# Vision-transformer layer on one core: the attention output turned ahead of the fourth unit, the second QKV product after it

## The chip, the cores and the metric

One core of a Trainium2 chip runs the whole kernel in one launch. The metric is the time of that launch in microseconds (us); the kernel before was run three times: 829.83 us median, 829.82 to 830.21. One execution was profiled.

The engines are named as in the profile: PE (TensorE, matmuls and transposes), PEld (its weight loads), DVE (VectorE), ACT (ScalarE), POOL (GpSimd), SP (SyncE, which issues nearly all DMAs).

## What is computed

32 images of 3 x 224 x 224 are cut into 256 patches each and embedded to 256 features (x). Then one layer follows: attention with a causal mask (16 heads of 16 features, 4 key and value heads) on the normalised x, added to x, and a feed-forward part with quantised activations and weights.

```python
h = tok(x)                                   # patches @ W + b
h = h + attn(layernorm(h))                   # causal, 16 heads, 4 kv heads, rotary positions
h = h + ffn(layernorm(h))                    # int8-like fake quantisation, silu(gate) * up, down
# attn: q, k, v = x@wq, x@wk, x@wv; q, k rotated
#       softmax(mask(q k^T / 4)) v, then @ wo
```

The quantisation scale of the feed-forward part is the largest magnitude over all images, so all images must be through attention before the feed-forward part starts. The change lies in the first part, attention.

## The kernel before

The first part is a pipeline over images, written as one step function for each engine (PE, ACT, POOL, DVE, SP), called for each step x from -3 to 34. Steps 6 to 27 run in a hardware loop, two steps a turn; the others are written out. In one step several images are at work at once: the patch product of image x+3, the QKV product of x+2 (in two halves of 128 tokens), the units of x+1, the first four score pairs of image x and the last four of x-1, and the output product of x-2. Each engine runs its step function in the written order. The engines meet only through semaphores, so an instruction that waits holds up all that stands behind it on its engine.

The work that the change and the prediction name, in the order in which one image meets it:

- *patch* (PE L484): the embedding, two halves of 15 matmuls. ACT scales it and makes a 16-bit high part (L767, L772), DVE the low part of h (L1204), SP turns both by a DMA transpose (L380).
- *QKV product*, `project(x, 0)` and `project(x, 1)` (PE L498): 6 matmuls for each half of the tokens. ACT converts each half (L791), POOL rotates it (L991, L994) and adds (L1004). ACT then makes the maximum stack (L807, L809) and, after one exponential, the score stack (L820 to L822), DVE its low part (L1184, L1186).
- *unit*, `unit_pair` 0 to 5 (PE L516 or L522, and L535), and *maximum*, `reduce_pair` 0 to 5 (DVE L1198): a first pass over the scores that finds each row's maximum. A unit waits for the maximum before it, since they share two banks. The units are here called first to sixth. They need the transposed maximum stack (SP L388).
- *score pair* 0 to 7 (PE L550, L552), and its exponential (ACT L829). All score pairs share one pair of banks, so score pair i waits for the exponential i-1. The first four need the first two of four DMA transposes of the score stacks (SP L400), which in turn wait for all six maxima of that image. The first to fourth are score pairs 0 to 3.
- *mask* (POOL L979) of each exponential, and *attend* 0 and 1 (PE L566, L570): probabilities times values. ACT copies its result out (L837).
- *turn*, `o_turn(x, 0)` and `o_turn(x, 1)` (PE L581): four transposes each of image x-1's attention output into a bank of 512 columns each. DVE takes the reciprocal of the sums (L1237) and divides (L1245): this is `o_sums` and `o_normalise`. ACT makes the high part (L844), DVE the low part (L1263), SP turns both (L410).
- *output product*, `out_project` (PE L591), and the residual (DVE L1255).

Four kinds of job share two banks, `shared[0]` and `shared[1]`. `JOBS` lists them in PE's order, the place in the list modulo 2 gives the bank, and `PLACE` says which image a step does. `take_bank` derives from the list what a job must wait for: the job two places earlier in the list must have been read out.

```python
JOBS = [("patch", 0), ("out", 0), ("qkv", 0), ("qkv", 1), ("o_t", 0), ("o_t", 1)]
PLACE = {("patch", 0): 3, ("out", 0): -2, ("qkv", 0): 2, ("qkv", 1): 2, ("o_t", 0): -1, ("o_t", 1): -1}
```

So before, patch waits for the reading of the turn's first half (the division), out for that of the second half, the second QKV half for the residual, and the turn for the conversions of the QKV product. The division reads both banks at once and counts for both halves.

ACT's order in a step, which the change leaves alone (`late` is the image whose exponentials run; the fourth exponential is `exp_pair(late, 3)`):

```python
exp_pair(late, 0); o_copy(late + -1, 1); values(late); projected(late, 0)
exp_pair(late, 1); projected(late, 1)
exp_pair(late, 2); exp_pair(late, 3)
x_high(early); on_high(late); high(late); exp_pair(late, 4); fill_stack(late)
```

SP's order in a step, unchanged too: load of the next patches, transposes of h (L380), of the attention output (L410), of the maximum stack (L388), four of the score stacks (L400), and the store of h1 (L365).

Of the kernel before, what the change touches and what calls it, by code (L numbers as in the profile page):

```python
# [30 lines left out]
D = 256  # L31
# [81 lines left out]

JOBS = [("patch", 0), ("out", 0), ("qkv", 0), ("qkv", 1), ("o_t", 0), ("o_t", 1)]
PLACE = {("patch", 0): 3, ("out", 0): -2, ("qkv", 0): 2, ("qkv", 1): 2, ("o_t", 0): -1, ("o_t", 1): -1}
PER_IMAGE = {"patch": 1, "qkv": 2, "o_t": 2, "out": 1}

# [1 line left out]
def vit_layer(nc, x_t, w_emb, w_qkv, w_o, w_gate, w_up, w_down, clips, rope, eye, tri, out):  # L121
    with ExitStack() as ctx:
# [332 lines left out]
        def _(pe):  # L455
# [34 lines left out]
            def project(x, tb):  # L490
                z = x + 2
                b = take_bank(z, ("qkv", tb))
                pe.wait_ge(h_turned[z.parity], z.half * 16 + 16)
                if x.known and z.n == 0 and tb == 0:
                    pe.wait_ge(weights_split, 3)
                for c in range(DC):
                    for sx, sw in PARTS:
                        mm = pe.matmul(b[:, 0:QKV_COLS], h_t[:, sx, tb, c, :], wqkv[:, sw, c, :],  # L498
                                       start=(c == 0 and (sx, sw) == PARTS[0]),
                                       stop=(c == DC - 1 and (sx, sw) == PARTS[-1]))  # L500
                mm.then_inc(done["qkv"], 1)
# [82 lines left out]
            def out_project(x):  # L584
                w = x + -1
                b = take_bank(w, ("out", 0))
                pe.wait_ge(on_turned[w.parity], w.half * 16 + 16)
                for tb in range(TB):
                    for c in range(DC):
                        for sx, sw in PARTS:  # L590
                            mm = pe.matmul(b[:, tb * D:(tb + 1) * D], on_t[:, sx, tb, c, :],  # L591
                                           wo[:, sw, c, :], start=(c == 0 and (sx, sw) == PARTS[0]),
                                           stop=(c == DC - 1 and (sx, sw) == PARTS[-1]))
                mm.then_inc(done["out"], 1)
# [38 lines left out]
            def step(x):  # L633
                early, late = x + 1, x + -1
                if (x + 3).exists():
                    patch(early, 0)
                if (x + -1).exists():
                    score_pair(late, 4)
                if x.exists():
                    unit_pair(late, 5)  # L640
                if (x + 3).exists():
                    patch(early, 1)
                if (x + -1).exists():
                    score_pair(late, 5)
                    attend(late, 0)
                    score_pair(late, 6)
                if (x + -2).exists():
                    out_project(late)
                if (x + 1).exists():
                    unit_pair(x, 0)  # L650
                if (x + -1).exists():
                    score_pair(late, 7)
                if x.known and x.n == -2:
                    turn_weights(0)
                if (x + 2).exists():
                    project(x, 0)
                if x.exists():
                    score_pair(x, 0)
                if (x + 1).exists():
                    unit_pair(x, 1)  # L660
                if (x + -1).exists():
                    attend(x + -1, 1)
                if x.known and x.n == -2:
                    turn_weights(1)
                if (x + 1).exists():
                    unit_pair(x, 2)
                if x.exists():
                    score_pair(x, 1)
                if (x + 2).exists():
                    project(x, 1)  # L670
                if x.exists():
                    score_pair(x, 2)
                if (x + 1).exists():
                    unit_pair(x, 3)
                if (x + -1).exists():
                    o_turn(x, 0)
                    o_turn(x, 1)
                if x.known and x.n == -2:
                    turn_weights(2)
                if x.exists():  # L680
                    score_pair(x, 3)
                if (x + 1).exists():
                    unit_pair(x, 4)
# [413 lines left out]
        def _(dve):  # L1097
# [135 lines left out]
            def o_sums(x):  # L1233
                w = x + -1
                dve.wait_ge(done["o_t"], w.n * 2 + 2)
                o = pair[0][:, :].rearrange("p (b h d) -> p b h d", b=TB, h=HEADS)
                dve.reciprocal(sums, o[:, :, :, HD:HD + 1]).then_inc(sums_ready, 1)  # L1237
# [66 lines left out]
            def step(x):  # L1304
# [17 lines left out]
                    norm_stats(early)  # L1322
                if (x + 1).exists():
                    reduce_pair(x, 2)
                if (x + 3).exists():
                    h_low(early)
                if x.known and x.n == -2:
                    quantise_weights(2)
                if (x + 1).exists():
                    reduce_pair(x, 3)  # L1330
                if (x + -1).exists():
                    o_sums(x)
                    o_normalise(x)
                if (x + 1).exists():
                    reduce_pair(x, 4)
                if x.known and x.n == -2:
# [160 lines left out]
```

## Time and profile before

| | |
|---|---|
| median of three runs | 829.83 us |
| profiled execution | 827.3 us |
| its span, first to last instruction | 825.6 us |
| mean granted TensorE clock | 0.954 of full (full is 2.4 GHz) |
| busy: PE, DVE, ACT, POOL | 666.7, 663.3, 586.9, 591.5 us |

The first part takes about 650 us of the span, the feed-forward part the rest. A row of a timeline gives the start and the duration in us, the engine, the line, the operation, the output and the input, how often it is repeated, and in brackets how long the engine sat idle just before and what ended the wait. A duration ends a little after the next instruction of the same engine may start, since they are pipelined.

### The profile page before, as it was taken

What the parts mean: (1) busy time and instruction counts of PE and PEld (TensorE: products, weight loads), DVE (VectorE), ACT (ScalarE), POOL (GpSimd) and SP (SyncE); (2) the same over time, 40 slices, a digit from 0 to 9 for tenths busy, and PEclk for the clock granted to TensorE, in tenths of its full rate; (3) what the DMA queues carried; (4) which work ended last, traced back from release to release, by engine and by line L of the source; (5) the groups of instructions that cost most, each with busy time, mean ns of one, the idle gap of its engine ahead of it and who ended that gap; (6) DMA issues with size and microseconds to landing.
All of it is one profiled execution on the core that took longest, in us unless ns stands there. A gap on an engine that the chain in (4) does not pass through costs nothing. (4 is left out here: it accounts for less than half of the span.)

```text
span 825.6 us, 20928 instructions
## 1 busy us (share of the span) xinstructions
PE 666.7 (81%) x6706; PEld 381.5 (46%) x6706; DVE 663.3 (80%) x1052; ACT 586.9 (71%) x972; POOL 591.5 (72%) x689
## 2 busy tenths in 40 slices
PE   3578888888888888888888888888776369997894
PEld 2344555554555555545555555455333223332563
DVE  5856888888888888888888888888765359999894
ACT  4346677777777777787777777877666258886883
POOL 1456888888888888888888888886654148884363
PEclk9797999999999999999999999999889769999898
DMA  8245666667666655566665655665543212221499
GB/s 278 58 97 114 127 138 135 123 135 138 140 134 146 143 133 121 132 139 140 134 144 144 133 121 132 140 140 103 104 77 62 61 38 52 49 40 25 71 177 160
DMA packets 245384, 96.57 MB, mean 117 GB/s; under 512 B 222432, under 2 KB 240608, under 8 KB 245344
## 3 DMA queue, kind: packets, MB, share of 16 engines
q1 hardware_dynamic: 236896, 87.69, 48.3%
q0 software_dynamic: 8448, 8.39, 6.9%
q8 instruction: 20, 0.33, 0.2%
q14 instruction: 20, 0.16, 0.1%
HBM read 24.74 MB, written 16.78 MB: 50 GB/s over the span
## 5 line engine op out<-in xcount | busy, mean ns | idle before, releaser
L1198 DVE TENSOR_REDUCE act_all<-pair 128x4 f16<-128x1024 f32 (+1 forms) x192 | 234.2, 1220 | 34.5 <-PE pair L535 34.4
L484 PE MATMUL pair<-act_all 128*128 128x256 f16 (+1 forms) x960 | 116.7, 275 | 21.1 <-DVE act_all L1245 18.5
L829 ACT ACTIVATE act_all<-pair 128x768 f32<-128x768 f32 x128 | 103.0, 805 | 32.2 <-PE pair L552 32.2
L979 POOL TENSOR_SCALAR_AFFINE_SELECT ffn<-ffn 128x512 f32<-128x512 f32 x128 | 93.8, 742 | 42.4 <-ACT ffn L829 39.6
L829 ACT ACTIVATE ffn<-pair 128x768 f32<-128x768 f32 x128 | 102.1, 797 | 19.1 <-PE pair L552 19.1
L979 POOL TENSOR_SCALAR_AFFINE_SELECT act_all<-act_all 128x512 f32<-128x512 f32 x128 | 78.4, 633 | 43.2 <-ACT act_all L829 43.2
L484 PEld LDWEIGHTS pair<-act_all 128*128 128x128 f16 (+1 forms) x960 | 90.1, 98 | 40.0 <-issue 22.6
L550 PE MATMUL pair<-act_all 64*128 64x256 f16 x512 | 72.6, 280 | 39.7 <-ACT ffn L829 24.3
L1184 DVE TENSOR_TENSOR act_all<-act_all 128x512 f16<-128x512 f32 x32 | 69.8, 2181 | 41.2 <-ACT act_all L822 41.2
L991 POOL TENSOR_TENSOR act_all<-act_all 128x160 f32<-128x160 f32 x128 | 76.4, 618 | 27.2 <-ACT act_all L791 27.2
L1011 POOL TENSOR_TENSOR act_all<-act_all 128x1280 f16<-128x1280 f32 x31 | 81.4, 2627 | 18.0 <-ACT act_all L781 18.0
L498 PE MATMUL pair<-act_all 128*128 128x384 f16 x384 | 76.4, 337 | 0.0
L1004 POOL TENSOR_TENSOR act_all<-act_all 128x320 f32<-128x320 f32 x64 | 68.1, 1064 | 10.8 <-POOL act_all L994 10.5
L940 ACT ACTIVATE ffn<-pair,gate_scale 128x512 f32<-128x512 f32 x96 | 60.9, 653 | 16.2 <-PE pair L710 9.0
L550 PEld LDWEIGHTS pair<-act_all 64*128 64x128 f16 x512 | 24.9, 93 | 99.5 <-ACT ffn L829 50.6
L837 ACT ACTIVATE act_all<-pair 128x512 f32<-128x512 f32 x64 | 38.0, 593 | 41.6 <-PE pair L570 41.6
L1018 POOL TENSOR_TENSOR act_all<-act_all 128x2 f32<-128x2 f32 x64 | 44.6, 698 | 27.2 <-DVE act_all L1283 19.4
L522 PE MATMUL pair<-act_all 64*128 64x256 f16 x512 | 50.0, 274 | 15.0 <-DVE act_all L1198 13.7
L535 PE MATMUL pair<-act_all,eye_wide 64*128 64x128 bf16 (+1 forms) x768 | 60.3, 236 | 0.0
L807 ACT ACTIVATE act_all<-act_all 128x512 f16<-128x512 f32 x32 | 20.2, 630 | 53.2 <-POOL act_all L1004 53.2
L591 PE MATMUL pair<-act_all 128*128 128x256 f16 x384 | 50.1, 283 | 8.8 <-DMA act_all<-ffn 8.8
L552 PE MATMUL pair<-act_all 64*128 64x128 f16 x512 | 56.9, 219 | 0.0
(135 smaller groups left out, 1510.9 us busy)
## 6 DMA issues: line engine op xcount, KB each, us to landing
act_all<-x_t SPq DMA_DIRECT2D x32, 640.0 KB, 4.2
out<-act_all SPq DMA_DIRECT2D x32, 256.0 KB, 2.6
out<-ffn POOLq DMA_DIRECT2D x16, 512.0 KB, 7.0
act_all<-act_all SPq DMA_TRANSPOSE x192, 3.0
act_all<-w_down SPq DMA_DIRECT2D x1, 704.0 KB, 8.4
act_all<-w_emb SPq DMA_DIRECT2D x1, 640.0 KB, 3.9
ffn<-w_gate SPq DMA_DIRECT2D x1, 640.0 KB, 6.9
ffn<-w_up SPq DMA_DIRECT2D x1, 640.0 KB, 7.5
```

Of the source, the lines that this page charges most:

```text
L484: mm = pe.matmul(b, xs[0:k, sx, c, tb * P:(tb + 1) * P], we[0:k, sw, c, :], start=(c == 0 and (sx, sw) == PARTS[0]), stop=(c == KC - 1 and ...
L498: mm = pe.matmul(b[:, 0:QKV_COLS], h_t[:, sx, tb, c, :], wqkv[:, sw, c, :], start=(c == 0 and (sx, sw) == PARTS[0]), stop=(c == DC - 1 and ...
L535: mm = pe.matmul(on_diagonal, eye_wide[rows, at_:at_ + P], tri_b[rows, rows].rearrange("p (a t) -> p a t", a=1).to_broadcast([64, n_, 64]) ...
L550: pe.matmul(b[:, 0:TOKENS], op[rows, k, 0:P], op[rows, pair_, :], start=True, stop=True)
L829: act.activation(probs[i // 4][:, o:o + 2, 0:3, :].rearrange("p h k s -> p h (k s)"), pair[1][:, :].rearrange("p (h c) -> p h c", h=2)[:, ...
L940: act.activation(silu[m % 3][:, 0:cols], bank[2 + m % 3][:, 0:cols], ACT.Silu, scale=gate_scale[:, m:m + 1]).then_inc(silu_ready, 1)
L979: pool.affine_select(out=p, in_=p, pattern=[[0, 4], [1, P]], compare_op=ALU.is_ge, fill=0.0, base=0, channel_multiplier=-1).then_inc(maske ...
L991: op = pool.tensor_tensor(rot_b[:, at_, :, to], qk_of_qkv[:, at_, :, of], rope_s[:, 1, at_, :, to].to_broadcast([P, 1, QK, 8]), ALU.mult)
L1004: pool.tensor_tensor(qk[:, tb].rearrange("p h d -> p (h d)"), rot_a[:, tb].rearrange("p h d -> p (h d)"), rot_b[:, tb].rearrange("p h d -> ...
L1011: pool.tensor_tensor(x_parts[v.parity][:, 1], xt[v.parity], x_parts[v.parity][:, 0], ALU.subtract).then_inc(x_low_ready, 1)
L1184: dve.tensor_tensor(stack[:, :, 0:HEADS, 32:48], qk[:, :, 0:HEADS, :], stack[:, :, 0:HEADS, 16:32], ALU.subtract)
L1198: dve.tensor_reduce(to, pair[2][:, :].rearrange("p (k g t) -> p k g t", k=2, g=n_), AX.X, ALU.max).then_inc(unit_reduced, 1)
```

## The change

The list of jobs has the second QKV half at its end. With it the turn's first half gets bank 1 and its second half bank 0, so the two halves of the tokens lie in the other order, and the output product reads `1 - tb` to put them right. The turn's first half now waits for the residual, its second half for the conversion of the first QKV half, and the second QKV half for the division; patch waits for the division too, and out for the conversion of the second QKV half. PE's order becomes: score pair 1, turn, score pair 2, fourth unit, second QKV half, score pair 3. On DVE, the reciprocal and the division come before the low part of h and the fourth maximum. ACT, POOL and SP are not touched.

```diff
-JOBS = [("patch", 0), ("out", 0), ("qkv", 0), ("qkv", 1), ("o_t", 0), ("o_t", 1)]
+JOBS = [("patch", 0), ("out", 0), ("qkv", 0), ("o_t", 0), ("o_t", 1), ("qkv", 1)]
@@ out_project
-                            mm = pe.matmul(b[:, tb * D:(tb + 1) * D], on_t[:, sx, tb, c, :],
+                            mm = pe.matmul(b[:, tb * D:(tb + 1) * D], on_t[:, sx, 1 - tb, c, :],
@@ PE, step
                     score_pair(x, 1)
+                if (x + -1).exists():
+                    o_turn(x, 0)
+                    o_turn(x, 1)
+                if x.exists():
+                    score_pair(x, 2)
+                if (x + 1).exists():
+                    unit_pair(x, 3)
                 if (x + 2).exists():
                     project(x, 1)
-                if x.exists():
-                    score_pair(x, 2)
-                if (x + 1).exists():
-                    unit_pair(x, 3)
-                if (x + -1).exists():
-                    o_turn(x, 0)
-                    o_turn(x, 1)
@@ DVE, step
                     reduce_pair(x, 2)
+                if (x + -1).exists():
+                    o_sums(x)
+                    o_normalise(x)
                 if (x + 3).exists():
                     h_low(early)
                 if x.known and x.n == -2:
                     quantise_weights(2)
                 if (x + 1).exists():
                     reduce_pair(x, 3)
-                if (x + -1).exists():
-                    o_sums(x)
-                    o_normalise(x)
```

## Rows read from the trace of the kernel before

**Rows 1.** Waits of PE from 106 to 565 us: who waited for whom, sum, times, longest.

```profile
PE pair L484 <- DVE act_all L1245: 17.4, 25, 0.7
PE pair L550 <- ACT ffn L829: 15.1, 50, 0.4
PE pair L516 <- DVE act_all L1198: 9.5, 21, 0.5
```

**Rows 2.** One step: length; busy PE, PEld, DVE, ACT, POOL (instructions); clock; DMA share, GB/s.

```profile
403.93:422.31 18.38, 16.08 (x185) 9.63 (x184) 15.74 (x27) 14.25 (x25) 15.59 (x20) 1.00 0.60 136
```

**Rows 3.** Timeline of PE in that step: start, duration, engine, line, operation [idle before].

```profile
411.51 0.28 PE L550 MATMUL pair<-act_all 64*128 64x256 f16 x2
...
412.30 0.40 PE L516 MATMUL pair<-act_all 64*128 64x128 f16 x8 [0.45 <-DVE act_all L1198]
...
415.16 1.15 PE L498 MATMUL pair<-act_all 128*128 128x384 f16 x6
416.63 0.28 PE L550 MATMUL pair<-act_all 64*128 64x256 f16 x2 [0.33 <-ACT act_all L829]
...
417.23 1.09 PE L581 MATMUL pair<-act_all 128*128 128x128 f32 x8
418.26 0.28 PE L550 MATMUL pair<-act_all 64*128 64x256 f16 x2
...
418.63 0.39 PE L522 MATMUL pair<-act_all 64*128 64x256 f16 x4
...
419.86 1.80 PE L484 MATMUL pair<-act_all 128*128 128x256 f16 x15 [0.72 <-DVE act_all L1245]
```

**Rows 4.** Timeline of ACT in that step.

```profile
415.30 0.58 ACT L791 ACTIVATE act_all<-pair,act_all 128x384 f32<-128x384 f32 x1
...
418.64 0.81 ACT L829 ACTIVATE act_all<-pair 128x768 f32<-128x768 f32 x1 [0.81 <-PE pair L552]
...
420.50 0.62 ACT L844 ACTIVATE ffn<-act_all 128x512 f16<-128x512 f32 x1
422.69 0.63 ACT L807 ACTIVATE act_all<-act_all 128x512 f16<-128x512 f32 x1 [1.57 <-POOL act_all L1004]
```

**Rows 5.** Timeline of DVE in that step.

```profile
416.27 0.83 DVE L1204 TENSOR_TENSOR act_all<-act_all 128x512 f16<-128x512 f16 x1
...
418.49 0.35 DVE L1237 RECIPROCAL act_all<-pair 128x32 f32<-128x32 f32 x1
418.93 0.69 DVE L1245 TENSOR_TENSOR act_all<-pair,act_all 128x512 f32<-128x512 f32 x1
...
421.16 0.69 DVE L1263 TENSOR_TENSOR ffn<-act_all,ffn 128x512 f16<-128x512 f32 x1 [0.40 <-ACT ffn L844]
```

**Rows 6.** Timeline of POOL in that step: rotation of the second half, and its addition.

```profile
419.30 1.00 POOL L991 TENSOR_TENSOR act_all<-act_all 128x160 f32<-128x160 f32 x2
...
421.29 1.28 POOL L1004 TENSOR_TENSOR act_all<-act_all 128x320 f32<-128x320 f32 x1 [0.17 <-POOL act_all L994]
```

**Rows 7.** Timeline of SP's DMA issues; last, the first two L400 transposes' landing.

```profile
421.88 1.23 SPq L410 DMA_TRANSPOSE act_all<-ffn  x1
423.64 1.42 SPq L388 DMA_TRANSPOSE act_all<-act_all  x1
425.22 5.45 SPq L400 DMA_TRANSPOSE act_all<-act_all  x4
...
DMA to landing us min/median/max: 2.8/2.9/3.0
```

**Rows 8.** Line L1184 of DVE over the whole span, and POOL's masks in that step.

```profile
L1184 DVE TENSOR_TENSOR act_all<-act_all x32: 691/2442/2819, 44.1 to 608.9; 128x512 f16<-128x512 f32 x32
...
422.52 1.81 POOL L979 TENSOR_SCALAR_AFFINE_SELECT act_all<-act_all 128x512 f32<-128x512 f32 x3
```

**Rows 9.** Two long waits late in PE's timeline.

```profile
588.41 0.40 PE L550 MATMUL pair<-act_all 64*128 64x256 f16 x2 [2.62 <-ACT ffn L829]
...
627.91 1.47 PE L591 MATMUL pair<-act_all 128*128 128x256 f16 x12 [1.83 <-DMA act_all<-ffn]
```

More of the change, by code:

```diff
@@ L668, in step @@
                     score_pair(x, 1)
-                if (x + 2).exists():
-                    project(x, 1)
+                if (x + -1).exists():
+                    o_turn(x, 0)
+                    o_turn(x, 1)
                 if x.exists():
@@ L674, in step @@
                     unit_pair(x, 3)
-                if (x + -1).exists():
-                    o_turn(x, 0)
-                    o_turn(x, 1)
+                if (x + 2).exists():
+                    project(x, 1)
                 if x.known and x.n == -2:
```

## The prediction

> **What bounds the kernel now.** The change touches only the first part of the program, the loop over 32 images, so I read there. First, the waits of TensorE in the steady stretch [rows 1]: 25 waits for the division in 459 us, so a step takes 459 / 25 = 18.36 us. Second, one such stretch by engine [rows 2]: TensorE is busy 16.08 us of 18.38 and no other engine over 15.8. No engine is full; TensorE idles 2.3 us in pieces. So the step is set by a ring of waits, and the timelines of the engines show it.
>
> The ring of before: first maximum (VectorE) releases the second unit at 412.30, the second attend follows, ScalarE copies its output, converts the first QKV product (415.30), GpSimd rotates both halves until 422.57, ScalarE's next operation starts at 422.69 and had been free since 421.12 [rows 3, 4, 6]; the fifth exponential, the stack fill, VectorE's low parts and the residual follow, and then the next first maximum. Two things the change touches stand outside it: the patch product waits 0.72 us for the division at 419.86, and the third score pair waits 0.33 us for an exponential at 416.63 [rows 3].
>
> **The change, part by part.** Nothing is added or removed; the turned output's halves change banks and the output product reads them crosswise, which costs nothing (same instructions, same sizes). No DMA is added. Two program orders and three bank waits change.
>
> (1) *The turn comes first.* It takes the place where the second QKV product started, 415.16 [rows 3]. The eight transposes take 1.09 us [rows 3]. The second four now take the bank of the first QKV product, which ScalarE has read at 415.30 + 0.58 = 415.88 [rows 4]. Half of 1.09 plus the drain of one is 0.65: end 416.55. TensorE would then have waited for the exponential until 416.63 anyway, so the turn itself costs nothing here.
>
> (2) *The division.* VectorE is done with the third maximum when its next operation starts, 416.27 [rows 5], so it waits for the turn. Reciprocal at 416.60; the division starts 0.44 later and takes 0.69 [rows 5], ending at 417.73. The low part of h and the fourth maximum are queued behind it, some 1.2 us later each; the next that needs that maximum is the fifth unit, which (4) makes late anyway.
>
> (3) *The product has a new wait.* Its bank is now the one the division reads. The third score pair and the fourth unit in front of it end by 417.23 [rows 3], so TensorE waits for 417.73. Between the division's end (418.93 + 0.69 = 419.62) and the patch product (419.86) lie 0.24 us [rows 3, 5]; I take 0.2. The product runs 417.95 to 419.10, 1.15 us long and 2.8 us later than before (415.16).
>
> (4) *What is queued behind it on ScalarE.* ScalarE's order is not changed: it converts the second product and only then runs the third exponential, which releases the fourth score pair. Conversion at 419.17, 0.58 long; the exponential behind it takes 0.81 [rows 4], so 419.75 to 420.56; the score pair at 420.6 instead of 418.26 [rows 3]. TensorE stands still from 419.10 to 420.6, about 1.5 us: this stall is new. The patch wait of 0.72 goes in return, for the division is long done. From score pair to patch product it was 1.60 with that wait, so 0.88 without: 421.5 instead of 419.86, TensorE 1.6 us late.
>
> How much of this reaches the ring? Three ways lead to the next second unit.
>
> TensorE's own: of the 2.3 us of idle time, 0.72 and 0.33 lie ahead of the patch product; the other 1.25 lie behind it, and of them (15.1 + 9.5) / 25 = 1.0 ahead of the second unit, as waits for exponentials and for the first maximum [rows 1]. 1.6 less 1.0 is **0.6 us a step**.
>
> ScalarE's: the fourth exponential 0.38 after its scores, at 421.0 (before 418.64); the copy of the output's high part 1.86 later (418.64 to 420.50), at 422.84, to 423.46; so the operation that started at 422.69 starts 0.52 behind its start, at 423.35 [rows 4]. GpSimd's second rotation could begin at 419.75 instead of 419.30 [rows 6] and stays covered by this. **0.65 us a step**, straight into the old ring.
>
> SyncE's queue: the low part of the output waits for the high part: 423.5 instead of 421.16 on VectorE, 0.69 us [rows 5], ended 424.2. SyncE issues the output's transpose then (424.24, was 421.88), and it takes the queue for 1.23 us. The transpose for the maximum stack comes behind it and one more check of semaphores: 425.6 instead of 423.64. The four of the score stacks come 1.58 behind that (423.64 to 425.22), 427.2; the second of them at a quarter of 5.45 later, 428.55, and it lands after 2.9: 431.45 [rows 7]. The next first score pair needs it. Before, it started at 411.51 + 18.36 = 429.87 [rows 3], and the same sum gave a landing at 429.5: cover of 0.4 us. Now it starts at 431.5, the second unit 0.37 later (as 418.26 to 418.63), 431.87 against 412.30 + 18.36 = 430.66 [rows 3]: **1.2 us a step**. This is the longest of the three, and it closes on itself: second unit, attend, turn, division, product, conversion, third exponential, output transpose, stack transposes, first score pair. A ring of 19.6 us.
>
> A rule of the skill bears on this term. What the rows show: VectorE's subtraction for the score stack's low parts took 0.69 us at its shortest and 2.44 at the median [rows 8]; in the steady steps GpSimd's long subtraction of the next patches runs beside it, and in the last steps, where it is short, that one is missing. The output's low part, a subtraction of the same kind, moves from 421.16 to 423.5, among GpSimd's three masks of 0.6 us each, which start at 422.52 [rows 5, 8]. The Trainium skill, SBUF — State Buffer, section "SBUF: two separate sides", states that a VectorE instruction with two SBUF inputs and a GpSimd instruction that reads SBUF exclude each other, and the later one waits for the whole of the other. By it the ring would be up to 0.6 us longer, 1.8 instead of 1.2, when a mask has just begun. Without it I keep 1.2 and put 0.3 more into the range.
>
> **The sum.** Steps 1 to 29 have both a turn and a product. 27 of them at 1.2 are 32.4. The last two have no new image to widen between the fourth exponential and the output's high part, so that way is shorter, and steps -1 and 0 move the product behind the fourth unit without a turn: these four lie between 0 and 1.2, I take 0.8 (ScalarE's way costs 0.65 without SyncE's): 3.2. Together 35.6. The last three steps have no QKV product; the turn comes up to 1 us earlier in them, where the output product waits for its transpose; I count 0, at best -1. The profiled execution took 827.3 us (span 825.6), so 862.9; the median of the runs shown, 829.8, lies 2.5 above it: **865 us**, slower by 4.3%.
>
> **The rivals.**
> *Only the short ways count.* If the stack transposes land early enough (their cover is worked out from few rows, and 0.6 us would do it), a step costs 0.6: 27 x 0.6 + 3 = 19, so 849 us. For it: two ways agree on it. Against: SyncE's queue has three transposes behind one late one. Chance 0.2.
>
> *The clock falls.* TensorE's granted clock went from 2.4 to 1.2 GHz around waits of 2.62 us late in the loop, and there a score matmul took 0.40 us instead of 0.28 [rows 3, 9]. Against: a wait of 1.83 us left it up, for the 12 matmuls behind it took 1.47 us, 0.12 each, as the patch product's 15 in 1.80 [rows 3, 9], and the new stall is 1.5. Each fall would double a few us of work, of which perhaps 2 show. One fall in every second or third step adds 18 to 27 to the 865: 883 to 892. Chance 0.1.
>
> *Hidden.* If the third exponential's delay is taken up by waits that I have not seen, nothing changes: 830. Against: the queue orders force the stall, and rows show at most 1.25 us of slack behind it. Chance 0.04.
>
> *Faster.* If the second product did not have to wait, the patch wait (0.72 us) is the only large steady TensorE wait and would be gone: 27 x 0.5 = 14, so 816. It decides where the product starts: only if that is before about 416.7, so that the third exponential ends by the time the fourth unit does (417.3), is there no stall. The reciprocal cannot start before 416.5 by the rows, and the ring of before does not run through the patch wait. Chance 0.07.
>
> The forecast itself (1.0 to 1.5 a step, 859 to 874) has 0.5; the rest, 0.09, is in between.
>
> **Range and chances.** Low end at the short ways, 847; high end at the longer ring (1.8 a step: 27 x 0.6 = 16 more, 881) and part of the clock's case: 885. A measurement tells 0.2% (1.7 us) apart. Faster 0.07, same 0.04, slower 0.89.
>
> **What would show it.** The fourth score pair waits about 1.5 us for ScalarE's third exponential in each step, the second product waits about 0.5 us for the division, the patch product waits for it no more; the first score pair (or the first unit) waits for a DMA in nearly every step; a step takes 19.5 us. If the fourth score pair has no such wait, step (4) is wrong. If it has, but no wait for a DMA appears, the short ways hold. A granted clock under 1.00 in the steady stretch is the clock's case. The prediction fails wholly if the step stays at 18.36.

## The result and the profile after

| | before | after |
|---|---|---|
| median of three runs | 829.83 us (829.82 to 830.21) | 875.46 us (872.26 to 875.65) |
| profiled execution, span | 827.3, 825.6 us | 875.46, 873.7 us |
| mean granted TensorE clock | 0.954 | 0.938 |

The change makes the kernel slower: ratio 1.0542, with a 95% interval of 1.0516 to 1.0568. The forecast was 865, so its direction and mechanism can be tested against the rows below, and 10 us of size are to be explained.

One step of the kernel after, in the same columns as [rows 2]:

```profile
416.04:435.74 19.70, 16.08 (x183) 9.64 (x184) 16.11 (x26) 14.29 (x25) 15.34 (x20) 1.00 0.56 126
```

The same work, to the hundredth on TensorE (16.08 us), in 19.70 us instead of 18.38. The clock is full. On TensorE only waiting has grown. The waits of TensorE from 106 to 590 us in the kernel after (who waited for whom, sum, times, longest):

```profile
PE pair L550 <- ACT act_all L829: 33.0, 24, 1.4
PE pair L591 <- DMA act_all<-ffn: 13.0, 22, 2.0
PE pair L498 <- DVE act_all L1245: 12.5, 24, 0.5
PE pair L550 <- DMA act_all<-act_all: 9.2, 21, 2.2
PE pair L516 <- DMA act_all<-act_all: 8.0, 19, 0.5
PE pair L581 <- ACT act_all L791: 4.6, 21, 0.2
```

Against [rows 1]: the patch product (L484) waits for the division no more. Instead a score pair waits 33.0 / 24 = 1.4 us for an exponential in every step, the QKV product waits 0.5 for the division, and there are three waits for DMAs in nearly every step; the kernel before has four such waits in its whole steady stretch, 2.3 us together. Where they lie, in TensorE's timeline of that step:

```profile
423.34 1.49 PE L591 MATMUL pair<-act_all 128*128 128x256 f16 x12 [0.34 <-DMA act_all<-ffn]
...
425.23 0.40 PE L516 MATMUL pair<-act_all 64*128 64x128 f16 x8 [0.40 <-DMA act_all<-act_all]
...
427.50 0.28 PE L550 MATMUL pair<-act_all 64*128 64x256 f16 x2 [0.41 <-DMA act_all<-act_all]
...
427.68 0.39 PE L516 MATMUL pair<-act_all 64*128 64x128 f16 x8
...
433.22 1.15 PE L498 MATMUL pair<-act_all 128*128 128x384 f16 x6 [0.52 <-DVE act_all L1245]
435.74 0.28 PE L550 MATMUL pair<-act_all 64*128 64x256 f16 x2 [1.37 <-ACT act_all L829]
...
436.34 1.81 PE L484 MATMUL pair<-act_all 128*128 128x256 f16 x15
```

The output product, the first unit and the first score pair each wait for one of SyncE's transposes: of the output (L410), of the maximum stack (L388), of the score stacks (L400). The second unit is at 427.68, the product is 433.22 to 434.4, and then TensorE stands 1.37 us before the fourth score pair. Why is seen on ScalarE:

```profile
434.40 0.58 ACT L791 ACTIVATE act_all<-pair,act_all 128x384 f32<-128x384 f32 x1 [2.43 <-PE pair L498]
434.88 0.80 ACT L829 ACTIVATE act_all<-pair 128x768 f32<-128x768 f32 x1
436.12 0.81 ACT L829 ACTIVATE act_all<-pair 128x768 f32<-128x768 f32 x1 [0.44 <-PE pair L552]
...
437.99 0.62 ACT L844 ACTIVATE ffn<-act_all 128x512 f16<-128x512 f32 x1
438.51 0.62 ACT L807 ACTIVATE act_all<-act_all 128x512 f16<-128x512 f32 x1
```

ScalarE idles 2.43 us in front of the conversion of the second half, while the third exponential, whose scores are long there, is queued behind it. The division and the output's low part on VectorE, and SyncE's queue:

```profile
432.47 0.69 DVE L1245 TENSOR_TENSOR act_all<-pair,act_all 128x512 f32<-128x512 f32 x1
...
438.64 1.00 DVE L1263 TENSOR_TENSOR ffn<-act_all,ffn 128x512 f16<-128x512 f32 x1 [0.96 <-ACT ffn L844]
```

```profile
421.29 1.50 SPq L388 DMA_TRANSPOSE act_all<-act_all  x1
422.96 5.50 SPq L400 DMA_TRANSPOSE act_all<-act_all  x4
...
439.67 1.23 SPq L410 DMA_TRANSPOSE act_all<-ffn  x1
441.00 1.45 SPq L388 DMA_TRANSPOSE act_all<-act_all  x1
```

**Where the 48.1 us of span went.** I cut the span at the 32 starts of the division (L1245), one a step. The first starts at 91.99 instead of 88.5: +3.5. The next 27 steps take 535.37 instead of 494.9: +40.5. The four steps behind them, to the last division, take 69.92 instead of 65.35: +4.6. What is left behind the last division is 0.4 shorter. Of the 40.5, a typical step in the hardware loop (the median) takes 19.62 us where it took 18.35, so 27 x 1.27 = 34.3; the other 6.2 come mainly from three steps, starting at 111.53, 152.92 and 194.35, that take 21.5 to 21.8 us each. The first two are written out, the third is the first step of the hardware loop. In the first of them SyncE's queue reads:

```profile
118.73 1.23 SPq L410 DMA_TRANSPOSE act_all<-ffn  x1
120.06 2.49 SPq L388 DMA_TRANSPOSE act_all<-act_all  x1
```

and TensorE behind it:

```profile
123.59 2.38 PE L591 MATMUL pair<-act_all 128*128 128x256 f16 x12 [1.98 <-DMA act_all<-ffn]
```

The output's transpose lands 4.7 us after its issue there, and 3.2 to 3.3 us in the loop; the next transpose occupies the queue for 2.49 us instead of 1.50. TensorE waits 1.98 us instead of 0.34, and then its granted clock is down for some 3 us: the twelve matmuls of the output product take 2.38 us instead of 1.49. The second of the three is the same (4.7 us, and a wait of 2.00). In the third it is the four transposes of the score stacks that take 6.74 us on the queue instead of 5.50, and the first score pair waits 2.17 us; there the clock stays up.

What runs beside such a transpose stands in the same trace. The DMA queues from 119 to 123 us (queue and kind, packets, MB, share of 16 engines):

```profile
q1 hardware_dynamic: 1361, 0.34, 101.6%
q8 instruction: 1, 0.02, 1.6%
```

The second line is one transfer of 16 KB on a queue of the kind "instruction". It starts at 120.95, inside the transpose of 2.49 us; in the other two steps one starts at 162.45 and at 208.26, again inside the slow transpose. From 219 to 620 us, in the loop, this queue moves nothing. In the eleven profiles of this case, from 80 to 720 us, 74 transposes stay on SyncE's queue for more than 1.6 us, and 61 of them overlap such a transfer; of the 2243 others 60 do. The kernel before has it too: one of its score stack transposes takes 1.93 us at 187.93, with such a transfer at 187.84, and that step is 18.65 us long. There SyncE's queue has cover; after the change it has none. This is a coincidence in time, seen in every run. No run moves these transfers alone, so that they cause the delay is likely and not shown.

### The profile page after: what moved, and what is told of

The parts are those of the page before. It is cut to its first block and busy times, and to the rows that moved or that the text cites. A ratio compares the mean times of both kernels' runs of the same rounds, so it can differ in the third digit from the quotient of the medians.

```text
span 873.7 us, 20928 instructions
## 1 busy us (share of the span) xinstructions
PE 683.7 (78%) x6706; PEld 390.0 (45%) x6706; DVE 673.3 (77%) x1052; ACT 587.4 (67%) x972; POOL 588.9 (67%) x689
## 5 line engine op out<-in xcount | busy, mean ns | idle before, releaser
L829 ACT ACTIVATE ffn<-pair 128x768 f32<-128x768 f32 x128 | 102.7, 802 | 53.6 <-PE pair L552 53.6
L484 PE MATMUL pair<-act_all 128*128 128x256 f16 (+1 forms) x960 | 124.1, 286 | 4.5 <-POOL act_all L1011 3.3
L979 POOL TENSOR_SCALAR_AFFINE_SELECT act_all<-act_all 128x512 f32<-128x512 f32 x128 | 91.9, 741 | 47.3 <-ACT act_all L829 47.3
L829 ACT ACTIVATE act_all<-pair 128x768 f32<-128x768 f32 x128 | 103.2, 806 | 23.9 <-PE pair L552 22.6
L484 PEld LDWEIGHTS pair<-act_all 128*128 128x128 f16 (+1 forms) x960 | 93.7, 102 | 26.3 <-issue 7.3
L991 POOL TENSOR_TENSOR act_all<-act_all 128x160 f32<-128x160 f32 x128 | 64.9, 528 | 44.7 <-ACT act_all L791 44.7
L791 ACT ACTIVATE act_all<-pair,act_all 128x384 f32<-128x384 f32 x64 | 37.2, 581 | 85.6 <-PE pair L498 79.0
L1184 DVE TENSOR_TENSOR act_all<-act_all 128x512 f16<-128x512 f32 x32 | 68.4, 2136 | 4.7 <-ACT act_all L822 4.6
L1004 POOL TENSOR_TENSOR act_all<-act_all 128x320 f32<-128x320 f32 x64 | 62.5, 977 | 10.8 <-POOL act_all L994 9.4
L591 PE MATMUL pair<-act_all 128*128 128x256 f16 x384 | 52.6, 292 | 20.4 <-DMA act_all<-ffn 20.4
L1018 POOL TENSOR_TENSOR act_all<-act_all 128x2 f32<-128x2 f32 x64 | 44.0, 700 | 21.8 <-DVE act_all L1283 14.1
L522 PE MATMUL pair<-act_all 64*128 64x256 f16 x512 | 50.9, 278 | 9.0 <-DVE act_all L1198 8.9
```

The source lines that it names most:

```text
L484: mm = pe.matmul(b, xs[0:k, sx, c, tb * P:(tb + 1) * P], we[0:k, sw, c, :], start=(c == 0 and (sx, sw) == PARTS[0]), stop=(c == KC - 1 and ...
L829: act.activation(probs[i // 4][:, o:o + 2, 0:3, :].rearrange("p h k s -> p h (k s)"), pair[1][:, :].rearrange("p (h c) -> p h c", h=2)[:, ...
L979: pool.affine_select(out=p, in_=p, pattern=[[0, 4], [1, P]], compare_op=ALU.is_ge, fill=0.0, base=0, channel_multiplier=-1).then_inc(maske ...
L991: op = pool.tensor_tensor(rot_b[:, at_, :, to], qk_of_qkv[:, at_, :, of], rope_s[:, 1, at_, :, to].to_broadcast([P, 1, QK, 8]), ALU.mult)
L1004: pool.tensor_tensor(qk[:, tb].rearrange("p h d -> p (h d)"), rot_a[:, tb].rearrange("p h d -> p (h d)"), rot_b[:, tb].rearrange("p h d -> ...
L1184: dve.tensor_tensor(stack[:, :, 0:HEADS, 32:48], qk[:, :, 0:HEADS, :], stack[:, :, 0:HEADS, 16:32], ALU.subtract)
```

## The experiments

Nine kernels. "Step" is the typical spacing of the division in the hardware loop (before 18.35, after 19.62). Ratios are against the kernel before on the same chip, whose medians there were 828.65 (the first four), 828.01 (the next three) and 829.57 us (the last two).

| kernel | edit | median us | ratio, 95% | step us |
|---|---|---|---|---|
| e1 | after, third exponential before the conversion | 843.29 | 1.0171 (1.0134 to 1.0208) | 18.61 |
| e2 | before, only the second product moved | 846.31 | 1.0206 (1.0169 to 1.0243) | 18.73 |
| e3 | after, output's high part before the widening | 849.87 | 1.0245 (1.0207 to 1.0284) | 18.81 |
| e4 | before, only VectorE's part | 910.65 | 1.0971 (1.0931 to 1.1011) | 20.8 to 22.2 |
| e5 | before, copy of the attend's output later | 818.89 | 0.9888 (0.9861 to 0.9914) | 17.80 |
| e6 | after, e1 and e3 together | 837.92 | 1.0105 (1.0077 to 1.0132) | 18.53 |
| e7 | after, VectorE's order of before | 946.67 | 1.1418 (1.1367 to 1.1470) | 22.19 |
| e8 | before, e5 and e3's edit | 816.65 | 0.9841 (0.9823 to 0.9859) | 17.85 |
| e9 | before, e3's edit alone | 824.35 | 0.9943 (0.9922 to 0.9963) | 18.16 |

**e1: is it the third exponential?** The kernel after, with the exponential taken out from behind the conversion of the second half:

```diff
@@ ACT, step (kernel after)
                     exp_pair(late, 1)
+                if (x + -1).exists():
+                    exp_pair(late, 2)
                 if (x + 1).exists():
                     projected(late, 1)
                 if (x + -1).exists():
-                    exp_pair(late, 2)
                     exp_pair(late, 3)
```

> The changed kernel with ScalarE's third exponential placed ahead of the conversion of the second QKV half. Theory (the stall comes from ScalarE's order, the product being late behind the division): the fourth score pair waits for ScalarE no more, a step falls from 19.62 us to between 18.4 and 18.8, and the time to 832 to 845 us. Rival (the price is the second product itself coming 2.8 us later, through GpSimd's rotation, whatever ScalarE's order): the step stays above 19.2 and the time above 860 us.

Measured: 843.3 us, step 18.61, both as expected. Of the 45.6 us between the two medians, 31 are gone by this one edit (843.29 is 14.6 above its own 828.65), so the late third exponential and what follows from it carry two thirds of the loss. The waits of TensorE from 220 to 560 us in e1 have no wait for L829 any more (VectorE's lines stand one lower down in this kernel: L1199 is the maximum, L1246 the division):

```profile
PE pair L522 <- DVE act_all L1199: 10.5, 37, 0.4
PE pair L498 <- DVE act_all L1246: 9.9, 19, 0.5
PE pair L550 <- DMA act_all<-act_all: 6.6, 18, 0.6
```

The wait for the division is still there, 0.5 us in every step. So what it holds up on TensorE itself is at most a small part of the loss; it counts by what it makes late on ScalarE.

**e2: the product's place alone.** The kernel before, with the old banks and the old place of the turn:

```diff
@@ PE, step (kernel before)
-                if (x + 2).exists():
-                    project(x, 1)
                 if x.exists():
                     score_pair(x, 2)
                 if (x + 1).exists():
                     unit_pair(x, 3)
+                if (x + 2).exists():
+                    project(x, 1)
```

> The kernel before with only the second QKV half moved behind the fourth unit; the turn, the banks and VectorE's order stay, so the product waits for no division. Theory (late product ahead of the third exponential is the cause, the wait for the division only lengthens it): the fourth score pair starts about 1.6 us later in the step, partly covered by the turn, and a step costs 0.4 to 0.6 us more: 841 to 848 us. Rival (only the new bank wait costs): 830 us.

Measured: 846.3 us, as expected, with a step 0.38 longer, just under the expected 0.4 to 0.6. A wait of 1.4 us for an exponential appears here too, and the patch product's wait for the division stays:

```profile
PE pair L550 <- ACT act_all L829: 25.0, 18, 1.7
PE pair L484 <- DVE act_all L1245: 12.7, 18, 0.7
PE pair L550 <- DMA act_all<-act_all: 7.2, 19, 0.9
```

This wait is not the stall of the kernel after. It lies ahead of the third score pair and is for the second exponential, which stands behind the conversion of the first QKV half. In the kernel before the second product filled that time, and 0.33 us of the wait were left [rows 3]; in the kernel after the turn fills it. The fourth score pair does not wait in e2: the turn lies between it and the product. So e2 costs 18 us by a late product and a gap that nothing fills, and how the 18 us divide between the two is not shown. The fourth score pair starts 7.45 us after the second unit, in the kernel before 5.96 [rows 3], in the kernel after 435.74 - 427.68 = 8.06. What the whole change adds to e2 is that the product also waits for the division, and with it the score pair is another 0.6 us later. The step grows by more, 0.38 here and 1.27 there. The two differ by the 0.6 and by the subtraction for the output's low part, which takes 0.69 us in e2 and 1.00 after: 0.6 + 0.3 = 0.9. That these sizes agree is an argument and not a test.

**e3: is the way from there SyncE's queue?** The stall stays, but the output's high part no longer stands behind 1.26 us of widening the next image:

```diff
@@ ACT, step (kernel after)
-                if (x + 4).exists():
-                    x_high(early)
                 if (x + -2).exists():
                     on_high(late)
+                if (x + 4).exists():
+                    x_high(early)
                 if (x + 1).exists():
                     high(late)
```

> The changed kernel with the output's high part ahead of the widening of the next patches on ScalarE, nothing else moved. Theory (the ring goes through the output's high and low part, the output's transpose and SyncE's queue): the output's transpose is issued about 1.2 us earlier in the step, the stack transposes 1.2 to 1.4 earlier, and the step falls by 0.6 to 0.7 us to the next shorter way, about 19.0: 856 to 860 us. Rival (TensorE's own lateness or GpSimd's rotation sets the ring): no change, 873 to 877 us.

Measured: 849.9 us, step 18.81, that is 0.81 us less than after. Both are better than expected (856 to 860 us, 0.6 to 0.7). The waits of TensorE from 220 to 560 us:

```profile
PE pair L550 <- ACT act_all L829: 24.7, 18, 1.4
PE pair L498 <- DVE act_all L1245: 9.4, 18, 0.5
...
PE pair L550 <- DMA act_all<-act_all: 2.1, 10, 0.3
```

The stall of 1.4 us is there in full, yet two thirds of the step's loss are gone, and so are most waits for DMAs. So most of the loss is not the stall on TensorE; it is what the late exponential does to the output's transpose, and through it to the transposes queued behind it.

**e4: VectorE's part alone.**

```diff
@@ DVE, step (kernel before)
                     reduce_pair(x, 2)
+                if (x + -1).exists():
+                    o_sums(x)
+                    o_normalise(x)
                 if (x + 3).exists():
                     h_low(early)
                 if (x + 1).exists():
                     reduce_pair(x, 3)
-                if (x + -1).exists():
-                    o_sums(x)
-                    o_normalise(x)
```

> The kernel before with only VectorE's part of the change: reciprocal and division ahead of h's low part and the fourth maximum. Theory (the patch product's wait for the division is not on the ring): that wait gets shorter or goes, the fifth unit waits for the fourth maximum in its place, and the time stays at 828 to 834 us. Rival (the patch wait counts): the step falls by 0.5 us, 816 us.

Measured: 910.7 us. This expectation missed wholly, and by far the most. VectorE and TensorE in one step of e4:

```profile
450.09 0.36 DVE L1237 RECIPROCAL act_all<-pair 128x32 f32<-128x32 f32 x1 [1.80 <-PE pair L581]
...
451.15 0.97 DVE L1204 TENSOR_TENSOR act_all<-act_all 128x512 f16<-128x512 f16 x1
452.04 1.22 DVE L1198 TENSOR_REDUCE act_all<-pair 128x4 f16<-128x1024 f32 x1
```

```profile
453.32 0.60 PE L522 MATMUL pair<-act_all 64*128 64x256 f16 x4 [3.00 <-DVE act_all L1198]
...
454.07 3.38 PE L484 MATMUL pair<-act_all 128*128 128x256 f16 x15
```

With the turn in its old place behind the fourth unit, VectorE waits 1.80 us for it, and the fourth maximum, whose scores are ready, stands behind the division and the low part of h. The fifth unit waits 3.0 us for that maximum in every step, and behind it the clock is down (0.50 granted from 453 to 459 us): the patch product takes 3.38 us instead of 1.80. So VectorE's part is only bearable together with the turn's move; the two are one edit.

**e7: the other half of that pair.** The kernel after, with VectorE's three lines put back:

```diff
@@ DVE, step (kernel after)
                     reduce_pair(x, 2)
-                if (x + -1).exists():
-                    o_sums(x)
-                    o_normalise(x)
                 if (x + 3).exists():
                     h_low(early)
                 if (x + 1).exists():
                     reduce_pair(x, 3)
+                if (x + -1).exists():
+                    o_sums(x)
+                    o_normalise(x)
```

> The changed kernel with VectorE's order as before (low part of h and fourth maximum ahead of reciprocal and division). Theory (the division releases the product and so is on the ring): division and product come 1.9 us later in the step, the step grows to 21.2 to 21.6 us, 918 to 930 us. Rival (the division's place on VectorE does not count, since the product is late for ScalarE's order alone): 873 to 878 us.

Measured: 946.7 us, more than expected. TensorE in one step of e7:

```profile
452.63 1.15 PE L498 MATMUL pair<-act_all 128*128 128x384 f16 x6 [2.37 <-DVE act_all L1245]
```

The product waits 2.37 us for the division, 1.85 more than after: that term was right. The step is 2.57 us longer, not 1.9, and the granted clock has fallen. The stretch from 252 to 565 us (columns as in [rows 2]) in e7, in e4 and in the kernel before:

```profile
252.00:565.00 313.00, 251.70 (x2554) 147.88 (x2554) 220.87 (x365) 202.35 (x352) 218.75 (x268) 0.88 0.49 112
```

```profile
252.00:565.00 313.00, 257.95 (x2653) 151.72 (x2653) 235.93 (x381) 211.46 (x366) 221.05 (x281) 0.90 0.51 116
```

```profile
252.00:565.00 313.00, 273.19 (x3110) 163.28 (x3105) 268.41 (x444) 243.14 (x427) 264.75 (x325) 1.00 0.59 133
```

Granted clock 0.88 and 0.90 where the kernel before has 1.00; in the kernel after it is 0.99. How much of e7's 22.19 us is the clock and how much the wait was not separated. Given where the product now stands, VectorE's new order is a repair that is worth some 70 us.

**e6: both repairs.** e1's and e3's edits in the kernel after.

> The changed kernel with both edits of the first two trials on ScalarE: the third exponential ahead of the conversion of the second QKV half, and the output's high part ahead of the widening. Theory (two rings are lengthened by the change, one through the stall and one through SyncE's queue, and each trial took one away): the waits for DMAs ahead of the first unit and the first score pair go, the step falls to 18.2 to 18.4 us as GpSimd's rotation sets it, and the time to 826 to 834 us. Rival (something else in the change costs 0.25 us a step, such as the fifth unit waiting for the fourth maximum): 840 us as with the first trial alone.

Measured: 837.9 us, step 18.53; expected were 826 to 834 and 18.2 to 18.4. No wait for a DMA is left in the loop, as expected, but the step is still 0.18 above before. The waits of TensorE from 220 to 560 us:

```profile
PE pair L522 <- DVE act_all L1199: 10.8, 38, 0.4
PE pair L498 <- DVE act_all L1246: 9.9, 19, 0.5
PE pair L516 <- DVE act_all L1199: 8.1, 18, 0.5
PE pair L550 <- ACT ffn L829: 7.3, 27, 0.3
```

The second unit waits for the first maximum again (L516), as in the ring of before [rows 3]; new beside it are the waits of L522 for maxima, the fourth being behind the division now. The profiled execution of e6 was the slowest of its four, 842.0 us, 14.7 above that of the kernel before. Of these, 3.1 lie ahead of the first division, 6.4 in the next 27 steps (27 x 0.18 is 5), and 5.4 in the last four (70.7 us, before 65.35). With every repair that I found on ScalarE the change still gains nothing.

**e5: the ring of before.** If the ring that the prediction read in the old kernel is right, shortening it must help where no wait is moved. ScalarE's copy of the second attend's output stands ahead of the conversion of the first QKV half, which that ring runs through:

```diff
@@ ACT, step (kernel before)
-                if (x + -2).exists():
-                    o_copy(late + -1, 1)
                 if x.exists():
                     values(late)
                 if (x + 1).exists():
                     projected(late, 0)
+                if (x + -2).exists():
+                    o_copy(late + -1, 1)
```

> The kernel before with one edit on ScalarE: the copy of the second attend's output placed behind the conversion of the first QKV half instead of ahead of it. Theory (the ring of before runs through second attend, copy, values, conversion, GpSimd's rotations, stack fill, low parts, first maximum): the conversion and all behind it come 0.49 us earlier in the step, the step falls by 0.3 to 0.5 us, and the time to 815 to 820 us. Rival (the step of before is set elsewhere, by TensorE's order or the turn, which now gets its input 0.9 us later): no change, 827 to 831 us, or slower.

Measured: 818.9 us, step 17.80, a ratio of 0.9888: faster than both kernels. The time is within what the ring said, and the step fell by 0.55, a little more than the 0.3 to 0.5.

**e8 and e9: the best version.** In e5 TensorE waits for the score stacks' transposes (7.1 us, 19 times), and e3's edit should free it. e8 has both; e9 is e3's edit alone, which was to show that on the old ring it does nothing.

> The kernel before with two edits on ScalarE: the copy of the second attend's output behind the conversion of the first QKV half (as in the trial before, 819 us, a step of 17.8 us in which the first score pair now waits 0.36 us for a DMA), and the output's high part ahead of the widening. Theory (with the first ring shortened, SyncE's queue sets the step, and it starts at the output's high part): the output's transpose is issued 0.85 us earlier in the step, the wait for the DMA goes, the step falls to 17.4 to 17.6 us, and the time to 810 to 814 us. Rival (the DMA wait is not what sets the step): 817 to 820 us.

> The kernel before with only the output's high part ahead of the widening on ScalarE. Theory (in the kernel before SyncE's queue is covered by 0.4 us and sets nothing): no change, 826 to 831 us, though the output's transpose is issued earlier. Rival (SyncE's queue is already on the ring before the change): the step falls by 0.5 us or more, 815 us.

Measured: e8 816.7 us, the fastest of all, but its step is 17.85, no shorter than e5's; e9 824.4 us, where no change was expected, with a step 0.2 us shorter. The DMA wait did go in e8: one wait of 0.2 us is left where e5 has nineteen. So e8 came out at its rival's size and e9 between its theory and its rival. Both misses have one likely cause, seen in GpSimd's addition behind the second rotation (L1004) and VectorE's subtraction beside it (L1263). In the kernel before, in e9, in e5 and in e8, in this order:

```profile
457.84 0.69 DVE L1263 TENSOR_TENSOR ffn<-act_all,ffn 128x512 f16<-128x512 f32 x1 [0.40 <-ACT ffn L844]
...
457.97 1.28 POOL L1004 TENSOR_TENSOR act_all<-act_all 128x320 f32<-128x320 f32 x1 [0.17 <-POOL act_all L994]
```

```profile
454.41 1.00 DVE L1263 TENSOR_TENSOR ffn<-act_all,ffn 128x512 f16<-128x512 f32 x1
...
455.03 1.10 POOL L1004 TENSOR_TENSOR act_all<-act_all 128x320 f32<-128x320 f32 x1 [0.17 <-POOL act_all L994]
```

```profile
449.94 0.86 POOL L1004 TENSOR_TENSOR act_all<-act_all 128x320 f32<-128x320 f32 x1 [0.17 <-POOL act_all L994]
```

```profile
448.74 1.27 POOL L1004 TENSOR_TENSOR act_all<-act_all 128x320 f32<-128x320 f32 x1 [0.17 <-POOL act_all L994]
```

The addition lies on the ring of before (ScalarE's next operation waits for it, [rows 4, 6]). It takes 0.86 us where nothing of VectorE's began ahead of it, 1.27 to 1.28 when the subtraction began 0.13 us ahead of it, and 1.10 when the subtraction began 0.6 ahead. The steady steps of each kernel repeat these sizes within 0.03 us. e9 shortens it by 0.18 and the step by 0.19. In e8 it is 0.41 longer than in e5, which takes back what the freed DMA wait would have given. That these two sizes agree is the ground for naming this cause; I made no run in which the two instructions are kept apart and all else stays.

## Why the prediction was right in its mechanism and short in its size

Direction, mechanism and range held (847 to 885). Times in the following comparison are counted from the second unit, which is at 412.30 in the rows before and at 427.68 in those after, since the two steps can't be laid over each other otherwise.

- *Step (1), the turn comes first and costs nothing.* The working counts three changed bank waits. There are four: the output product now waits for the conversion of the second QKV half. The rows show no wait of the output product for a bank, before or after, so this made no difference. The second half of the turn waits 0.2 us for the conversion that has to clear its bank. The exponential that was to cover this is not waited for any more. Small, as said.
- *Step (2), the division.* It ends at 433.16, 5.48 after the second unit; predicted 417.73 - 412.30 = 5.43. The dismissal of the delayed fourth maximum ("the fifth unit, which (4) makes late anyway") held here, but only because of (4): e4 shows the same order costing 3.0 us a step where the turn is late, and e1 and e6, in which (4) is repaired, show the L522 waits of 0.4 us for a maximum.
- *Step (3), the product waits for it.* It starts 5.54 after the second unit, predicted 5.65, with a wait of 0.52. In e2 the late place costs 0.38 us a step together with the gap described there; the other 0.9 comes with this wait and, as argued there, with what the subtraction then meets.
- *Step (4), the stall.* 1.37 us, predicted 1.5. The fourth score pair starts 8.06 after the second unit, predicted 8.3; the patch product 8.66, predicted 9.2. So TensorE is 1.1 us later than in the kernel before (7.56), not 1.6. I had carried over a spacing of 0.88 between score pair and patch product, and it is 0.60. I had also let the third exponential wait for the whole 0.58 us of the conversion; it starts 0.48 after the conversion's start.
- *Which way leads to the next step.* SyncE's queue, as chosen, against the rival of 0.2. The ring of after closes from the rows: second unit to the maximum stack's transpose 441.00 - 427.68 = 13.32 (predicted 13.3), to the score stacks' 1.67 (1.6), to the first score pair 427.50 - 422.96 = 4.54 (4.3), to the second unit 0.18 (0.37): 19.71 us, predicted 19.6. The 13.3 came out so well partly by luck: the output's high part started 0.23 us earlier than forecast (10.31 after the second unit instead of 10.54), and its low part took 0.31 us longer. e3 is the test of the way: with that way shortened by one operation and the stall left alone, the step falls by 0.81.
- *The next way down* was sized too long: ScalarE's was put at 0.65. The operation of [rows 4] that starts 10.39 after the second unit starts at 438.51, 10.83 after it, so +0.44, and e3, in which SyncE's waits are mostly gone, has a step 0.46 above before. The 0.2 is what the fourth exponential came earlier than forecast.
- *The rule on the two-input subtraction.* In the rows: the output's low part took 1.00 us instead of 0.69, and the three masks beside it 2.27 instead of 1.81. That agrees with what the Trainium skill, SBUF — State Buffer, section "SBUF: two separate sides", says of VectorE with two SBUF inputs against GpSimd, in that the later one waits. It cost 0.3, not the 0.6 of its worst case, and lay within the steps' 1.27.
- *The sum.* Against the profiled execution 862.9 was predicted and 875.46 measured, 12.6 too little, in three pieces. With it the time lies just above the 859 to 874 that had the chance of 0.5, though the step of 1.27 lies inside its 1.0 to 1.5. The steady step: 27 x 1.27 = 34.3 instead of 32.4, so 1.9. **The end steps, put at 3.2: 3.5 + 4.6 - 0.4 = 7.7, so 4.5.** This is the term that was argued by analogy, "between 0 and 1.2, I take 0.8", and not read; in the lead-out the score pair waits 1.02 us for the stack transposes at 677.84 and 0.9 to 1.0 three times for exponentials behind it, and the clock is down from 684 to 691. **The three early steps with a slow transpose: 6.2, with no term at all.** In the kernel before the waits for DMAs from 84 to 215 us add up to 1.6 + 0.5 = 2.1 us, in the kernel after to 6.4 + 3.2 + 1.7 = 11.3. The slow transposes coincide with the 16 KB instruction transfers shown above; the lead-out has three more, at 639.19, 659.06 and 671.25, each with such a transfer.
- *The rivals.* The clock's fall happened, but in the early steps with a 2 us wait and in two steps of the loop, not in every second or third: two falls in the loop made steps of 19.97 instead of 19.63. Full size it reached only in e4 and e7. The faster side had its condition right: the product would have had to start before 416.7, which is 4.4 us after the second unit, and it started 5.54 after it, 1.1 us too late.

## What to carry to other kernels

A stall on one engine is not the price of a change: follow it to the queue that is last into the next step. Here 1.4 us on TensorE cost at most 0.46 us a step where SyncE's queue was freed (e3), and 1.27 where the same delay passed through ScalarE's order into SyncE's queue of transposes. When an operation is moved later on one engine, look at what is queued behind its consumer on the next engine, for there the program order may have to move with it (e1: one moved exponential, 31 of 46 us). And give the steps at both ends a term of their own: here they held more than a quarter of the loss (7.7 + 6.2 of 48.1 us). In them the trace has transfers on the instruction queue, which the middle of the loop has not, and a change that takes away a queue's cover lays their delays open.

## What the runs showed that was not expected

- *Whoever starts first keeps its length.* VectorE's and GpSimd's two-input instructions lengthen each other by up to 0.4 us (0.86 to 1.28 us on GpSimd, 0.69 to 1.00 on VectorE), so an edit elsewhere that shifts them by 0.5 us changes the step by 0.2. The Trainium skill's section named above has the exclusion, by which the later one is blocked for the whole of the other. In the rows it is lengthened by 0.14 us less than that: the subtraction at 457.84 would end 0.56 us after the addition's start at 457.97, and the addition takes 0.42 longer. That this already lay on the ring of the kernel before, in [rows 6], I had overlooked.
- *A transpose can be slow.* 4.7 us to landing instead of 3.2 in two written-out steps of the kernel after, with the next transpose on the queue for 2.49 and 2.32 us instead of 1.5, and 6.74 us instead of 5.50 for four of them in the first step of the loop. Each had a 16 KB transfer of the instruction queue beside it. From 219 to 620 us there was neither: no such transfer, and no transpose over 1.6 us.
- *The granted clock fell in every step of the two kernels that have a wait of 2.4 to 3.0 us in every step.* With 3.0 us (e4) and 2.37 + 1.4 us (e7) the mean over the stretch is 0.90 and 0.88; with 0.5 + 1.4 us (after) it is 0.99. Behind the wait of 3.0 us in e4 TensorE is at 1.2 GHz from 453 to 459 us, and the patch product takes 3.38 us instead of 1.80. The length of one wait does not decide it alone: in the kernel after the clock fell behind waits of 1.98 and 2.00 us and stayed full behind one of 2.17 (at 210.92).
